# Attention on one core: the context products of units 2 and 10 of each pair moved behind the scores and row maxima of the next unit

## The reference

```python
q = (resid @ Wq).reshape(B, T, 32, 32); k, v = (resid @ Wk), (resid @ Wv)   # 8 key/value heads of 32
q, k = rotary(q), rotary(k)
att = einsum('bhgqd,bhkd->bhgqk', q, k) / sqrt(32)        # 4 query heads g share one key head h
att = where(causal, att, -inf)
probs = softmax(att, axis=-1)
ctx = einsum('bhgqk,bhkd->bhgqd', probs, v)
out = ctx @ Wo
```

## Time and profile before

| | |
|---|---|
| median of three runs | 1605.55 us (1603.5 to 1607.41) |
| the profiled execution | 1605.24 us, span 1603.5 us |
| PE busy in the span | 1551.8 us, 97% |
| DVE, ACT, POOL busy | 938.3, 587.7 and 621.0 us |
| scores, line 1395 | 768 instructions |
| context products, line 1410 | 1536 instructions |

### The profile page before, as it was taken

One profiled execution on the slowest core, in us unless ns is written; L12 is line 12 of the kernel. 1 busy time (PEld: TensorE's weight loads), 2 busy tenths in 40 slices (PEclk: granted clock), 3 DMA queues, 4 the chain that ended last, 5 costly groups with the idle time before them and its releaser, 6 DMA issues. The chain is left out here.

```text
span 1603.5 us, 26749 instructions
## 1 busy us (share of the span) xinstructions
PE 1551.8 (97%) x9440; PEld 1199.6 (75%) x9440; DVE 938.3 (59%) x2707; ACT 587.7 (37%) x1201; POOL 621.0 (39%) x403
## 2 busy tenths in 40 slices
PE   7999998999999789999999999999999999999999
PEld 7999998788888655555555555555468999999998
DVE  6544563646463387888888878887527333333333
ACT  4323323212120126666666656666633111111110
POOL 1322223434343306676777666667742011010100
PEclk8999999999999969999999999999999999999999
DMA  6332233333322444443333334342344131323221
GB/s 226 121 122 94 107 134 132 119 119 118 105 93 79 131 96 97 103 96 87 87 87 94 94 91 96 97 109 62 87 170 147 53 105 53 106 64 93 78 66 40
DMA packets 152312, 162.77 MB, mean 102 GB/s; under 512 B 41744, under 2 KB 110608, under 8 KB 151920
## 3 DMA queue, kind: packets, MB, share of 16 engines
q1 hardware_dynamic: 123600, 137.37, 29.7%
q10 hardware_dynamic: 28592, 23.86, 4.5%
HBM read 104.05 MB, written 61.90 MB: 103 GB/s over the span
## 5 line engine op out<-in xcount | busy, mean ns | idle before, releaser
L1479 ACT ACTIVATE at_probs<-ps 128x512 f32<-128x512 f32 (+3 forms) x768 | 324.0, 494 | 141.0 <-PE ps L1395 138.6
L1552 DVE CUSTOM_DVE_ANT_0 ps<-ps,at_score_mask 128x512 f32<-128x512 f32 (+3 forms) x512 | 290.8, 618 | 37.6 <-PE ps L1384 34.7
L1395 PE MATMUL ps<-at_qs,at_ks 98*128 98x512 f32 (+3 forms) x528 | 192.7, 391 | 8.4 <-ACT at_probs L1479 6.0
L328 POOL TENSOR_TENSOR f_x_ring<-f_x_ring,f_half_bias 128x1024 f32<-128x1024 f32 x32 | 77.3, 2416 | 312.9 <-DVE f_h L582 312.4
L1384 PE MATMUL ps<-at_ks,at_qs 96*128 96x512 f32 (+3 forms) x528 | 175.6, 368 | 11.7 <-DMA at_ks<-scr_k_hi 11.1
L1395 PEld LDWEIGHTS ps<-at_qs,at_ks 98*128 98x128 f32 x528 | 97.4, 193 | 116.8 <-ACT at_probs L1479 91.5
L1410 PE MATMUL ps<-at_probs,at_vs 128*32 128x512 f32 (+3 forms) x1536 | 162.7, 496 | 0.2 <-POOL at_probs L1308 0.2
L1330 POOL TENSOR_TENSOR at_added<-at_added,at_probs 128x2048 f32<-128x2048 f32 x32 | 148.2, 4631 | 2.3
L1552 DVE CUSTOM_DVE_ANT_0 ps<-ps,at_score_mask,at_part_max 128x128 f32<-128x128 f32 (+3 forms) x256 | 134.1, 557 | 13.0 <-issue 10.6
L48 PE MATMUL f_ps<-f_wt_hi,f_hT_hi 128*128 128x400 f32 (+1 forms) x384 | 134.2, 350 | 3.2 <-DVE f_hT_lo L586 3.2
L1308 POOL TENSOR_SCALAR_AFFINE_SELECT at_probs<-at_probs 128x512 f32<-128x512 f32 x128 | 82.1, 652 | 137.9 <-ACT at_probs L1479 137.9
(11 more groups left out here) (159 smaller groups left out, 3158.3 us busy)
## 6 DMA issues: line engine op xcount, KB each, us to landing
at_qs<-scr_q_hi SPq DMA_DIRECT2D x20, 512.0 KB, 6.4
f_x_ring<-in_L_attn_resid SPq DMA_DIRECT2D x16, 512.0 KB, 3.6
x<-f_x_ring SPq DMA_DIRECT2D x16, 512.0 KB, 2.7
early<-x SPq DMA_DIRECT2D x16, 512.0 KB, 3.3
scr_q_hi<-qkv_rope_hi ACTq DMA_DIRECT2D x32, 256.0 KB, 2.0
scr_q_lo<-qkv_rope_lo ACTq DMA_DIRECT2D x32, 256.0 KB, 2.3
scr_ctx_hi<-at_ctx_hi SPq DMA_DIRECT2D x32, 256.0 KB, 2.2
scr_ctx_lo<-at_ctx_lo SPq DMA_DIRECT2D x32, 256.0 KB, 2.5
```

The lines of the kernel that those rows point to most:

```text
L328: pool.tensor_tensor(x_ring[:, u, :], x_ring[:, u, :], half_bias[:], ALU.add).then_inc(bias_added, 1)
L1395: pe.matmul(score_ps[(u * G + g) % BANKS][:, 0:z - a], ks[:, nm, j * P:(j + 1) * P], qs[nm][0:KROWS + 2, half, g, a - half * HALF:z - half ...
L1479: act.activation(probs[:, u % PROBS, g, 0:z - a], score_ps[(u * G + g) % BANKS][:, 0:z - a], ACT.Exp, scale=SCALE).then_inc(exp_done, 1)
L1552: dve.tensor_tensor_reduce(out=src, in0=src, in1=mask, scale=1.0, scalar=part_max[:, g, own] if c else -3.0e38, op0=ALU.add, op1=ALU.max, ...
```

## The change

In the units ahead of those that close a half, units 2 and 10, TensorE does not issue the context products but goes on with the next unit. In units 3 and 11 it issues first the products of units 2 and 10, then the sums, then the products of units 3 and 11. No instruction, operand, semaphore or count is added or dropped, and no other engine's program changes.

```diff
                         for m, it in items:
                             slot_item(m, it, n == NG - 1)
+                    if u + 1 in LAST:
+                        continue
                     if u in LAST:
+                        products(n, u - 1)
                         sums(n, LAST[u])
                     products(n, u)
```

## The result

The changed kernel is slower: 1612.95 us as the median of twelve runs against 1605.78 of the kernel before, a ratio of 1.0043 with a 95% interval from 1.0028 to 1.0057. The forecast was 1610.1 and slower. The profiled execution took 1608.89 us with a span of 1607.2, 3.65 us more than the one before.

The account below looks back on a forecast made before the run. The prediction took PE's own instruction order to bound the kernel. Half 1's +6.2, half 0's -1.5 and the edges' +0.2 gave +4.9 us on 1605.24, so 1610.1 us, range 1605.5 to 1613.5.

Parts of the forecast that it names:

- PE's order sets the time: Attention stage: PE is in flight 401.35 of 405.30 us, so its time counts in full unless a wait absorbs it.
- A separate run costs 0.33 us of switching: At 31 places, a run of products that joins another saves 0.33 us if nothing waits.
- The wait at the fourth score of unit 11 gets longer by 0.6 to 0.8 us: Units 10 and 11: that score stays behind an idle PE for ACT, its wait about 0.6 to 0.8 us longer.
- Half 1 loses 0.44 a pair: Units 10 and 11: held products stand behind the unchanged wait, 0.44 us later in pairs 1 to 14, +6.2 us.
- Half 0 gains 0.11 a pair: Units 2 and 3: closing run begins 0.55 us sooner and is 0.44 longer; pairs 1 to 14, -1.5 us.
- The three edges, +0.2: Pair 0 in both halves and pair 15 in half 0, each between -0.33 and +0.44 us, +0.2 together.
- The sum, +4.9: Whole kernel: 6.2 - 1.5 + 0.2 = +4.9 us on 1605.24, giving 1610.1 us.
- only the switches count: Rival: all 31 joined runs gain 0.33 us, 10.2 in all, 1595.0 us; chance 0.06.
- half 0 in full: Rival: half 0 gains its full 0.33 us a pair while half 1 loses, +1.8 us, 1607.0; chance 0.17.
- both halves lose: Rival: half 0's fourth score also stays where it is, 28 x 0.44 + 0.2 = +12.5 us, 1617.7; chance 0.07.
- made up later: Rival: some 0.2 of half 1's 0.44 us returns in unit 0, 2.8 us less, 1607.3; chance 0.1.
- the prediction's estimate from it: Closing run: eight held products as two side-by-side packs, about 0.22 us, sum about 3 us lower; prediction decided against it.

Follow-up runs that it names:

- e9: Changed kernel with ACT's copy behind unit 11's exponentials, and exponentials from pair 1 on covering only half their queries: 1578.85 us, 0.9805.
- e8: Kernel before with ACT's copy behind unit 11's exponentials, and exponentials from pair 1 on covering only half their queries: 1585.98 us, 0.9849.
- e4: Kernel before, with POOL's division of half 0 moved ahead of the split of the Wo piece: 1601.67 us, 0.9972.
- e6: Changed kernel, with ACT's copy for half 0 moved behind the exponentials issued in unit 11: 1598.91 us, 0.9948.
- e3: Changed kernel, with POOL's division of half 0 moved ahead of the split of the Wo piece: 1607.51 us, 1.0013.
- e2: Kernel before, with only the products of unit 10 held back and unit 2 as before: 1614.98 us, 1.0066.
- e1: Kernel before, with only the products of unit 2 held back and unit 10 as before: 1608.17 us, 1.0012.
- e5: Kernel before, with ACT's copy for half 0 moved behind the exponentials issued in unit 11: 1602.85 us, 0.9972.
- e7: Kernel before, with the products of unit 8 held back to join those of unit 9, units 2 and 10 as before: 1611.03 us, 1.0033.

## Why the prediction was right

- *PE's order sets the time*: right. What PE lost in two stretches of each pair is found in the span, and the stretches between are unchanged to 0.02 us.
- *A separate run costs 0.33 us of switching*: right, 0.30 to 0.38 where nothing waits (e9 against e8).
- *The wait at the fourth score of unit 11 gets longer by 0.6 to 0.8 us*: wrong in size. The bracket grew by 0.35 us, because the second and third score were held up by ACT as well. The fourth comes 4.09 us behind the first score of unit 10, where it was 4.07, and that is what the forecast rests on.
- *Half 1 loses 0.44 a pair*: right, the median is 0.40. The chain from unit 6 through POOL and ACT to the fourth score was shown from both ends. With the division earlier (e4) the old wait of about 0.45 us goes, and with the copy behind the exponentials (e6) the hold costs nothing.
- *Half 0 gains 0.11 a pair*: right, 0.10, and it is ACT's pitch that takes the rest of the 0.33: the run began 0.53 us sooner, where the walk had 0.55.
- *The three edges, +0.2*: wrong in size. They came to 0.22 + 0.43 + 0.14 = 0.79. The largest is half 1 of pair 0, where I had no row for ACT. POOL is early there, but the copy stands between the exponentials all the same, and that alone holds the fourth score: with the division earlier (e3) pair 0 still loses 0.43, and with the copy later (e6) it does not (-0.05). The prediction says this of an early division ("bring half 1 only to even") but does not draw it for pair 0.
- *The sum, +4.9*: the closing stretches give 6.2 - 1.2 = 5.0 in the profiled executions. The medians are 7.2 us apart, with an interval of 4.5 to 9.2, so 4.9 is within it but low. That the stretches come to 5.0 is in part luck: pairs 1 to 14 of half 1 lost 5.7 us and not 6.2, and the edges 0.79 and not 0.2, two errors of about half a microsecond against each other.
- *The rivals*: "only the switches count" fell with e2, "half 0 in full" with e1, "both halves lose" with the table, and "made up later" with its rows between the halves.
- *The Trainium skill's page "TensorE: Matmul & The Clock Gate", section "Measured speedup vs the span model"*: by the prediction's estimate from it the held products would take 0.22 us; they took 0.45 (960.22 to 960.67). That does not show that the heads stand in line: eight products one after another, at the scores' 0.23 us for 512 columns, would take 0.92. Whether they overlap less than the estimate has it, or each takes longer, no run here shows.

**Still open** is where the rest of the median lies. The changed kernel's median is 2.2 us above what its closing stretches give, and those of e1, e2 and e3 are 2 to 4 us above. The held products are not what sets them apart, since e4 and e5 hold nothing back and show the same: e4 is 1.6 and e5 3.1 us above its stretches. In e6 and e7 it is about 1 us or less. The mean granted clock over the span was 0.9820 in the twelve runs of the changed kernel, 0.9818 and 0.9819 in e2 and e1, 0.9826 in e3 and e4 and 0.9827 in e5, against 0.9835 in the 29 runs of the kernel before beside e1 to e4; in e6 it was 0.9836. Among those 29 the time falls by 1.2 us for each 0.001 of clock, so 0.0015 would be 1.8 us. That is a correlation, and I tried nothing that sets the clock; why most of the edited kernels should have a little less of it than the kernel before is not known.

## What to carry to other kernels

Before moving work out from between two stretches, ask what was waited for behind it: here the products cost nothing where they stood, because a score behind them was held by a chain that began four units earlier, and behind that score they cost their full time. A saving per instruction shows only where no other engine sets the pitch, so walk the new order against the other engines' finishing times before counting it. The better edit was in the chain itself: one copy that the wait did not need, moved behind the work that PE was waiting for, was worth 0.48 us a pair (e5).

## What the runs showed of the hardware

The granted clock can fall in the middle of a dense stage, behind a short wait. In the profiled execution of the changed kernel with the late copy (e6), PE stood still in pair 12 for the DMA of the maxima's rows, and about 2 us later the granted clock fell to its lower level, 1.2 in place of 2.4 GHz. It was back after some 7 us. The wait and then two windows (the clock is the third figure from the end):

```profile
1036.82 0.73 PE L1395 MATMUL ps<-at_qs,at_ks 98*128 98x512 f32 x2 [1.17 <-DMA at_qs<-at_neg_lo]
```

```profile
1036.82:1038.63 1.81, 1.81 (x8) 1.23 (x8) 1.06 (x4) 1.22 (x3) 1.29 (x1) 1.00 1.06 250
...
1040.00:1043.00 3.00, 3.00 (x17) 1.59 (x19) 2.27 (x6) 1.65 (x3) 0.79 (x1) 0.50 1.08 221
```

That stretch, unit 2 to unit 4, took 3.08 us more than in the kernel before, where it is otherwise 0.09 less. In pair 15 the clock was at its lower level again (0.50 from 1151.8 to 1155.2), and the same stretch took 1.76 us more where the others took 0.14 or 0.15. The two, with the wait itself, are most of the 5.7 us by which this profiled execution (1604.65 us) is above the median of its seven runs (1598.91).

A wait of that kind does not always bring the clock down. In e2 PE stood 1.03 us at the same place of pair 12 for the same DMA, and the clock stayed at its upper level:

```profile
1045.60 0.73 PE L1395 MATMUL ps<-at_qs,at_ks 98*128 98x512 f32 x2 [1.03 <-DMA at_qs<-at_neg_lo]
```

```profile
1046.00:1049.00 3.00, 3.00 (x19) 1.73 (x18) 1.93 (x7) 2.39 (x5) 1.29 (x1) 1.00 1.08 220
1049.00:1052.00 3.00, 3.00 (x33) 1.24 (x35) 2.05 (x6) 1.74 (x4) 1.18 (x1) 1.00 1.10 225
```

So whether the wait brought the clock down in e6 is not shown.
